# Decay attention: the second pass without its mask product, later keys' weights cleared by GpSimd

## What is computed

```python
scores = jnp.einsum('bhid,bhjd->bhij', Q, K) / jnp.sqrt(jnp.float32(hd))
delta = ti[:, None] - ti[None, :]
causal = delta < 0
decay = jnp.where(causal, 0.0, -jnp.abs(deltaf) ** ALPHA)      # ALPHA = 1
scores = jnp.where(causal[None, None], -jnp.inf, scores) + decay[None, None]
attn = jax.nn.softmax(scores, axis=-1)
out = jnp.einsum('bhij,bhjd->bhid', attn, V)                    # then heads joined, out @ Wo.T + bo
```

## Time and profile before

| | before |
|---|---|
| time of three runs | 1366.42, 1359.74, 1363.04 us; median 1363.04 |
| span of the profiled execution, the only time shown of it | 1358.3 us |
| PE busy | 1079.5 us (79%) |
| DVE busy | 881.0 us (65%) |
| ACT busy | 685.8 us (50%) |
| POOL busy | 559.6 us (41%) |

### The profile page before, as it was taken

One profiled execution on the slowest core, in us unless ns is written; L12 is line 12 of the kernel. 1 busy time (PEld: TensorE's weight loads), 2 busy tenths in 40 slices (PEclk: granted clock), 3 DMA queues, 4 the chain that ended last, 5 costly groups with the idle time before them and its releaser, 6 DMA issues. The chain is left out here.

```text
span 1358.3 us, 25046 instructions
## 1 busy us (share of the span) xinstructions
PE 1079.5 (79%) x8292; PEld 708.4 (52%) x8292; DVE 881.0 (65%) x2989; ACT 685.8 (50%) x1268; POOL 559.6 (41%) x740
## 2 busy tenths in 40 slices
PE   8877777778189553299936999969977999899998
PEld 3222232336188553299934777744434777654544
DVE  6799999976455456377549888843648878840201
ACT  4786656644044301133206888737856888541221
POOL 4489988853633314544426444100025555100000
PEclk9799999998599765599978999989997999999999
DMA  2997000002422206211120000020612000000000
GB/s 63 206 202 126 0 1 0 1 0 71 140 61 57 92 7 219 70 41 44 37 74 1 2 3 3 2 53 6 203 47 89 3 2 3 2 1 0 16 0 16
DMA packets 85742, 66.77 MB, mean 49 GB/s; under 512 B 15102, under 2 KB 70412, under 8 KB 85612
## 3 DMA queue, kind: packets, MB, share of 16 engines
q1 hardware_dynamic: 79916, 53.65, 17.3%
q0 software_dynamic: 4544, 9.38, 1.9%
q10 hardware_dynamic: 1152, 2.10, 0.4%
HBM read 36.52 MB, written 28.59 MB: 48 GB/s over the span
## 5 line engine op out<-in xcount | busy, mean ns | idle before, releaser
L1076 POOL TENSOR_TENSOR hC<-h,Cs 128x1024 f32<-128x1024 f32 x64 | 150.8, 2356 | 35.3 <-DVE h L973 34.7
L786 PE MATMUL bank<-hC,ident 128*128 128x512 f32 x256 | 128.1, 624 | 45.1 <-POOL hC L1076 43.0
L973 DVE TENSOR_TENSOR_SCAN h<-bank,state,dBx 128x512 f32<-128x512 f32 x128 | 157.3, 1271 | 2.2
L1457 POOL DMA_INDIRECT moe_answers<-moe_yw,moe_xg x78 | 83.7, 1073 | 128.9 <-DVE moe_yw L1634 70.9
L2608 DVE CUSTOM_DVE_ANT_0 decay_below<-bank,decay_q_mask 128x256 bf16<-128x256 f32 x256 | 97.3, 419 | 23.3 <-PE bank L2420 22.4
L786 PEld LDWEIGHTS bank<-hC,ident 128*128 128x128 f32 x256 | 44.9, 192 | 103.9 <-POOL hC L1076 67.1
L2608 DVE CUSTOM_DVE_ANT_0 window_below<-bank,window_q_mask 128x192 bf16<-128x192 f32 x256 | 80.3, 353 | 28.6 <-PE bank L2420 27.0
L2548 ACT ACTIVATE decay_pb<-bank 128x512 f32<-128x512 f32 x128 | 76.2, 598 | 33.5 <-PE bank L2435 32.6
L885 ACT ACTIVATE bank<-dt,A 128x512 f32<-128x512 f32 x128 | 83.2, 683 | 18.7 <-DVE h L973 17.4
L1528 PE MATMUL bank<-moe_xgT,moe_wac 128*128 128x128 f32 x624 | 86.4, 284 | 6.5 <-issue 4.0
L1543 PE MATMUL bank<-moe_wd,moe_hT 128*128 x624 | 83.2, 278 | 5.7 <-DVE moe_hT L1621 2.5
(11 more groups left out here) (482 smaller groups left out, 2797.2 us busy)
## 6 DMA issues: line engine op xcount, KB each, us to landing
moe_slots<-blank SPq DMA_DIRECT2D x16, 1040.0 KB, 16.9
deep_rows<-token_weights SPq DMA_DIRECT2D x32, 256.0 KB, 3.9
moe_xg<-moe_slots SPq DMA_DIRECT2D x78, 65.0 KB, 1.9
moe_wa<-in_moe_w SPq DMA_DIRECT2D x2, 2048.0 KB, 9.7
moe_back<-moe_answers SPq DMA_DIRECT2D x8, 256.0 KB, 5.3
moe_back<-moe_answers ACTq DMA_DIRECT2D x8, 256.0 KB, 6.0
moe_wu<-in_moe_wu SPq DMA_DIRECT2D x1, 2048.0 KB, 15.4
deep_w<-in_deep_w SPq DMA_DIRECT2D x3, 512.0 KB, 6.5
```

What stands on the lines that cost most here:

```text
L786: last = nc.tensor.matmul(sum_bank(hh)[:], k.ident[:], hC[:, u % 2, hh, :], start=(n == 0), stop=(n == NS - 1))
L973: v.tensor_tensor_scan(h[:, u % 2, hh, :], decay_bank(u, hh)[:], dBx[:, u % 2, hh, :], state[:, n, hh:hh + 1], ALU.mult, ALU.add).then_inc ...
L1076: g.tensor_tensor(hC[:, u % 2], h[:, u % 2], Cs[:, u % 2, None, :].to_broadcast([P, H, CW]), ALU.mult).then_inc(q_hC, 1)
L1457: nc.gpsimd.indirect_dma_start(answers, bass.IndirectOffsetOnAxis(index, 0), yw[:, i % NY, :], None)\
```

## The change

`k_mask` and the mask matmul go, in the decay layer alone. The second pass then computes scores for later keys of the own tile too. To keep these bounded (their place columns would raise them with the distance), a second constant slot, `CONST + 1`, subtracts multiples of 256 where the key's block of 32 is behind the query's. After each exponential, POOL sets to zero, in `pb`, the weights of the later keys: `clear_future`, an affine select over 128 x 2 x 128 elements in place, 8 for each tile. `values` waits for these (semaphore `future_cleared`) and no longer for `ex`. POOL's work is written out in a fixed order with them: in the steps of tile y two selects, the split of tile y + 4, two selects, `lengths` of tile y + 3, four selects; the addition to X stands behind tile 0's.

```diff
@@ zeros (DVE), for i in 0, 1
+                yield
+                for j in range(1, 4):
+                    e.memset(self.qp[i][0:32 * j, :, C + 1, 3 * i + j - 1], 1.0)
+                    e.memset(self.kp[i][32 * max(j, 2):P, :, C + 1, 3 * i + j - 1], -2.0 * P)
+                e.memset(self.kp[i][32:64, :, C + 1, 3 * i], -2.0 * P)
+                yield
@@ masks (POOL)
-        yield from mask(self.k_mask, -1, ((BW, P), (P, 0)))
-        if not windowed:
+        if windowed:
+            yield from mask(self.k_mask, -1, ((BW, P), (P, 0)))
+        else:
@@ second_pass (PE)
-            masked(out)
+            if windowed:
+                masked(out)
...
-                                            q2[:, y % 2, g, 0:b - a], start=False, stop=(j == 1 and s == 1),
-                                            skip_group_check=True)
+                                            q2[:, y % 2, g, 0:b - a], start=(not windowed and j == 0 and s == 0),
+                                            stop=(j == 1 and s == 1), skip_group_check=True)
@@ values (PE)
-            pe.wait_ge(s_ex, y * G + 2 * m + 2)
+            pe.wait_ge(s_ex if windowed else s_low, y * G + 2 * m + 2)
@@ POOL
+        def clear_future(pool, y, w):
+
+            pool.wait_ge(s_ex, y * G + w + 1)
+            own_keys = pb[:, w % 4, :].rearrange("p (j q) -> p j q", j=2)[:, :, BW:HW]
+            nc.gpsimd.affine_select(out=own_keys, in_=own_keys, compare_op=ALU.is_ge, fill=0.0, base=0,
+                                    pattern=[[0, 2], [1, P]], channel_multiplier=-1).then_inc(s_low, 1)
...
+                lengths(pool, 0)
+                split(pool, nc.gpsimd, OWN)
+                lengths(pool, 1)
+                split(pool, nc.gpsimd, OWN + 1)
+                lengths(pool, 2)
+                for y in range(T):
+                    for w in range(G):
+                        if w == 2 and inside(y + 4):
+                            split(pool, nc.gpsimd, y + 4)
+                        if w == 4 and inside(y + 3):
+                            lengths(pool, y + 3)
+                        clear_future(pool, y, w)
+                    if y == 0:
+                        nc.gpsimd.tensor_tensor(X0[:], k.X[:], bo[:, None, :].to_broadcast([P, T, P]), ALU.add)\
+                            .then_inc(s_x0, 1)
```

More of the change, by code:

```diff
@@ L2166, in __init__ @@
         self.q_mask = sb("q_mask", [P, self.HW], BF16)
-        self.k_mask = sb("k_mask", [P, 2, self.MW], BF16)
+        self.k_mask = sb("k_mask", [P, 2, self.MW], BF16) if windowed else None
         self.place = None if windowed else sb("place", [P, 2])
@@ L2291, in columns @@
                 yield
-    MASKS = {True: 16, False: 15}
+    MASKS = {True: 16, False: 12}
     def ready(self, engine):
@@ L2343, in softmax_mixer @@
         s_longest = sem("longest")
+        s_low = None if windowed else sem("future_cleared")
         s_rot_v, s_rot_p, s_sp_v, s_sp_p = (sem(n) for n in ("rot_vector", "rot_pool", "split_vector", "split_pool"))
@@ L2766, in gpsimd @@
             m.ready(pool)
-            if not windowed:
-                lengths(pool, 0)
[L2769 to L2780, removed]
+            if windowed:
+                for y in range(OWN, T):
+                    rotate(pool, nc.gpsimd, y)
+                    split(pool, nc.gpsimd, y)
+            else:
+                lengths(pool, 0)
+                split(pool, nc.gpsimd, OWN)
[12 more added lines that the diff above has]
+                            .then_inc(s_x0, 1)
         yield Engines(sync, gpsimd, tensor, scalar, vector), vector_head
```

## The result

The changed kernel took 1374.53 us (1373.93 to 1375.81, 4 runs), the kernel before 1362.28 (1359.74 to 1366.42) beside it: ratio 1.0082, interval [1.0056, 1.0108]. The medians lie 12.3 us apart, the ratio stands for 11.2 (7.6 to 14.7). The forecast was 1375.0 in a range of 1366 to 1384. The profiled execution took 1373.93 us for a span of 1372.2, 13.9 above.

The account below looks back on a forecast made before the run. The prediction took PE's stream to set the pace before, and a loop through POOL's order after. It summed 10.9 - 1.6 + 2.7 = +12.0 us onto 1363.0, giving 1375.0 us, range 1366 to 1384.

Parts of the forecast that it names:

- The loop: Decay layer, second pass to second pass through POOL's selects, split and squares: 11.46 us a tile against 10.55, +0.91.
- the select: On POOL in the decay layer's tiles: each select takes 0.44 us, with bounds of 0.33 and 0.64.
- How many tiles pay: Decay layer, tiles 0 to 11, which have a split of tile y + 4: 12 x 0.91 = 10.9 us.
- The last four tiles: Decay layer, tiles 12 to 15, without a split: they win half of up to 3.4 us, 1.6.
- The addition to X: On POOL between tile 0's last select and tile 1's first: makes tile 1's selects late once, +2.7 us.
- Outside the layer: Expert layer before: 14 memsets on DVE and POOL's smaller mask work, costed at zero; 1 us for memsets without cover.
- Long selects: Rival: on `pb` a select takes what POOL's multiply takes, giving 1383 us; chance 0.10.
- Contention on DVE as a steady cost: Rival: six small DVE instructions a tile each wait out a select, adding 6 us, 1381; chance 0.07.
- The gain of 13.7 us: Rival: POOL finishes in time and the removed mask matmuls shorten PE's stream in full, 1349.3 us; chance 0.06.
- POOL almost never waiting between steps 1 and 4: Sign expected in the profile after, in the decay layer's steady part, where POOL's queue runs through selects and split.
- values of step 5 waiting for a select: Sign expected in the profile after: PE busy well below 96%, its step 5 values held by POOL's select.
- POOL's share: Sign expected in the profile after: POOL busy near 70% in the decay layer's steady part.

Follow-up runs that it names:

- E4: Changed kernel with only the squares of `lengths` moved ahead of the select of step 0 on POOL; ratio to before 1.0019, tiles 10.26 us.
- e9: Changed kernel with each select done twice, the second waiting for the first; ratio to before 1.0292, tiles 13.63 us.
- e3: Changed kernel with the addition to X cut into 16 pieces, one behind each tile's last select; ratio to before 1.0056.
- e1: Kernel before with only the 14 memsets of the second constant slot added; ratio to before 1.0013.
- e5: Changed kernel with POOL's order rewritten: `lengths` earlier, split in four parts between selects, addition to X in 16 pieces; ratio to before 0.9966.

## Why the prediction came out right

**The loop.** The mechanism was right. Forecast 11.46 us, measured 11.33, step by step with the times of the tile above (forecast in brackets): to the exponential 0.48 (0.49), to the next 1.40 (1.40), to the select 0.67 (0.68), the select 0.37 (0.44), the split 3.41 (3.37), two selects 0.73 (0.88), to the bias addition 0.75 (0.69), which takes 0.47 (0.47) to the maxima, to the reciprocal 0.69 (0.69), to the turned rows 0.63 (0.66), to the values 0.70 (0.66), to the turning of q 0.58 (0.57), to the next tile 0.45 (0.46). E4 shows by intervention that this chain was the one, and in e9 the same steps sum up to the tile again. What was off is the select: I added the register move of 29 ns to the row's 411 ns, where consecutive selects overlap by 0.04; three of them make 0.2 us a tile.

**How many tiles pay.** I gave all of tiles 0 to 11 the full surplus, 10.9 us. Measured on the copies, from tile 1 on without the addition's share: 6.8 us in ten intervals and 0.8 in tile 1's, and in front of them nothing (from the layer's first power to the first copy 45.6 us, 46.1 before). So this term was 3.3 us too large: the loop's 11.33 in place of 11.46 accounts for 1.6, and the rest is that the first tile paid nothing (0.8) and the first and last of the others paid less (10.89 and 10.78 in place of 11.33).

**The last four tiles.** Forecast -1.6, measured 31.2 - 32.8 = -1.6. "Half of 3.4" was a guess, and that it fits to a tenth is luck.

**The addition to X.** Forecast +2.7 and one tile of some 14 us; that tile took 15.84. Measured 5.3 of tile 1's interval less the 0.8 that every tile pays, 4.5; by e3 3.5 to 3.8. The step that failed was to walk only POOL's queue past it. The port that the Trainium skill describes (SBUF — State Buffer, the two sides of SBUF) was in my text as a rival for small selects, and its price on this one long instruction was not in the sum. The trace agrees with what the Trainium skill says, that the other waits for the whole instruction: the cast ended 0.06 us after the addition did.

**Outside the layer.** I costed the memsets at zero. The sum in the layer is 10.1 us by the profiles (steady -0.5 + 6.8 + 5.3 - 1.6), the measured difference of the medians is 12.3. The 2 us between would be outside (1 us by the ratio); e1 gives the memsets 1.8 (0.3 to 3.3), and PE's wait in the expert layer 1.0. That 1375.0 came so close to 1374.5 is thus luck in part: a term 3 us too large stood against two that were each some 2 us too small. The direction and the size of the surplus were not luck.

**The rivals.** Long selects: no, 402 to 413 ns. Contention on DVE as a steady cost: small casts were hit (the first of five has a median of 275 ns), yet in e5, where the five together take 1.1 us more, tiles are as short as without selects. The gain of 13.7 us: not even without selects (5.2), where waits for DVE and ACT take the rest. "POOL almost never waiting between steps 1 and 4" and "values of step 5 waiting for a select" came true; POOL's share, 69%, too.

## What to carry to other kernels

Before giving an idle engine a job that others wait for, write out its queue and look at what stands between the event that starts the job and the job: a share of busy time says there is room, the order says whether the room is where it is needed. Walk one period with measured durations through every wait that the new order adds, the side ones too (here the one for the squares, for which DVE had no wait before). And when a removed instruction was part of a full stream, look for the next two waits behind it; here moving them was worth more (0.59 us a tile in the kernel before) than the change (0.41 behind it). When a measured time looks like a round number of units, as 2.30 of 0.46, walk the timeline before counting them: a part of it can be the clock.

## What the runs showed of the hardware

A 16-column DVE cast between SBUF tiles took 3.55 us beside a GpSimd addition of 4.51 us. Behind 3.0 us without work in the changed kernel, and behind 2.6 us in each tile of e9, PE's matmuls ran at 1.2 GHz (granted 0.50) for some us, which in e9 costs 0.86 us a tile; with waits of some 0.8 us the changed kernel's steady tiles kept 1.00. Consecutive affine selects on GpSimd of 256 float32 elements a partition, in place over two separate runs of 128, start every 0.37 us and take 0.41. And the start of a layer, some 700 us into the program, lies up to 4 us apart in single profiles of kernels that are the same up to there (706.68 in e9, 710.73 in the changed kernel).
